# Last layer: one score and one peak side by side in TensorE's row halves, three PSUM banks for scores and four for peaks

## The reference, cut to what matters

```python
qkv = (x @ W_qkv + b_qkv).reshape(b, n, H, D, 3)          # b=64, n=1024, H=4, D=8
scores = jnp.einsum('bhnd,bhmd->bhnm', q, k) * scale
att = jax.nn.softmax(scores, axis=-1)
out = jnp.einsum('bhnm,bhmd->bhnd', att, v)
...                                                        # @ W_proj + b_proj, added to t
router_probs = jax.nn.softmax(x @ router_w + router_b, axis=-1)
top_p, top_i = jax.lax.top_k(router_probs, K)              # K=2 of 8 experts
```

## Time and profile before

| what | value |
|---|---|
| median of three runs | 6225.48 us (6224.43 to 6227.87) |
| the profiled execution, its own time | 6216.34 us |
| its span | 6214.5 us |
| mean granted TensorE clock | 0.956 |
| PE / DVE / ACT / POOL busy, whole span | 86% / 80% / 77% / 50% |

### The profile page before, as it was taken

The page is one execution under the profiler, slowest core; times in us unless marked ns, Lnnn a source line. Parts: engine busy times, 40 slices in busy tenths (PEclk is TensorE's granted clock), DMA queues, the critical chain, the costliest instruction groups (busy, mean ns, idle before and its releaser), DMA issues.

```text
span 6214.5 us, 145806 instructions
## 1 busy us (share of the span) xinstructions
PE 5346.4 (86%) x43064; PEld 2191.6 (35%) x43064; DVE 4957.7 (80%) x9330; ACT 4801.7 (77%) x8146; POOL 3128.8 (50%) x3692
## 2 busy tenths in 40 slices
PE   6649999999999998457999989998999899989997
PEld 5324444444444444442222222222222222222222
DVE  7837766767677675738999989999999899989995
ACT  1239989989899998215888888888888888888887
POOL 0037777777777776612444444444444344444443
PEclk9879999999999999677999999999999999999999
DMA  3010000000000000230000000000000000000000
GB/s 113 21 45 10 10 10 8 10 11 10 10 9 10 10 10 7 66 105 7 9 9 9 9 10 9 9 9 10 9 9 9 10 9 9 9 10 9 9 8 5
DMA packets 400111, 104.64 MB, mean 17 GB/s; under 512 B 348547, under 2 KB 398676, under 8 KB 398804
## 3 DMA queue, kind: packets, MB, share of 16 engines
q1 hardware_dynamic: 398163, 94.72, 7.1%
q10 hardware_dynamic: 1152, 0.05, 0.0%
HBM read 61.17 MB, written 33.56 MB: 15 GB/s over the span
## 4 chain that ended last, share of the span: by engine, by line
PE 24%; DVE 16%; issue 8%; ACT 3%; POOL 3%; DVEq 1%; DMA 0%; SPq 0%; ACTq 0%; POOLq 0%
DVE d_peaks L2296 12%; PE d_p_o L2124 7%; PE d_p_s L2111 5%; PE d_p_k L2140 5%; ACT d_wt L2007 2%; PE d_p_s L2213 2%; POOL d_rstd L1919 2%; PE d_p_s L2097 1%; PE d_p_s L2171 1%; PE d_p_s L2162 1%; DVE d_total L2306 1%; POOL d_xl L1923 1%; ACT d_answers L2003 1%; DVE d_rank L2388 1%; DVEq L2291 1%
## 5 line engine op out<-in xcount | busy, mean ns | idle before, releaser
L2296 DVE TENSOR_REDUCE d_peaks<-d_p_k 128x1 f32<-128x512 f32 x4096 | 2610.3, 683 | 242.8 <-PE d_p_k L2140 221.1
L2007 ACT ACTIVATE d_wt<-d_p_s 128x512 f32<-128x512 f32 x4096 | 2199.9, 616 | 416.0 <-PE d_p_s L2111 415.4
L771 ACT ACTIVATE b_wt<-b_sq 128x1024 f32<-128x1024 f32 (+3 forms) x1536 | 1240.0, 845 | 8.0 <-issue 8.0
L2124 PE MATMUL d_p_o<-d_wt,d_v_pad 128*32 128x512 f32 x8192 | 1095.5, 607 | 2.6 <-ACT d_o_sb L2012 1.9
L2140 PE MATMUL d_p_k<-d_kT,d_qT 64*128 64x512 bf16 x4096 | 800.8, 385 | 209.1 <-DVE d_peaks L2296 189.1
L680 POOL TENSOR_TENSOR b_sq<-b_sq 128x1024 f32<-128x1024 f32 (+1 forms) x512 | 849.6, 1680 | 234.4 <-DVE b_sq L995 234.4
L760 ACT ACTIVATE b_sq<-b_p_s 128x1024 f32<-128x1024 f32 (+2 forms) x1024 | 775.5, 757 | 180.2 <-PE b_p_s L831 173.3
L2111 PE MATMUL d_p_s<-d_qT,d_kT 64*128 64x512 bf16 x4096 | 801.4, 387 | 60.7 <-ACT d_wt L2007 40.4
L995 DVE TENSOR_TENSOR b_sq<-b_p_s,b_tri 128x1024 f32<-128x1024 f32 (+1 forms) x512 | 551.0, 1088 | 271.2 <-PE b_p_s L831 205.7
L1962 POOL TENSOR_TENSOR d_answers<-d_answers,d_mix 128x2048 f32<-128x2048 f32 x64 | 233.0, 3641 | 955.2 <-DVE d_mix L2397 955.2
L844 PE MATMUL b_p_o<-b_wt,b_v_pad 128*32 128x512 f32 (+2 forms) x6144 | 669.7, 508 | 1.9 <-ACT b_wt L771 1.0
(11 more groups left out here) (293 smaller groups left out, 7508.7 us busy)
## 6 DMA issues: line engine op xcount, KB each, us to landing
c_slots<-t SPq DMA_DIRECT2D x128, 128.0 KB, 2.5
a_xt<-in_x SPq DMA_DIRECT2D x4, 2048.0 KB, 14.7
a_w<-in_L_conv_W SPq DMA_DIRECT2D x64, 128.0 KB, 2.8
t<-a_rows SPq DMA_DIRECT2D x32, 256.0 KB, 2.4
b_x_in<-t SPq DMA_DIRECT2D x64, 128.0 KB, 2.7
t<-b_result SPq DMA_DIRECT2D x64, 128.0 KB, 2.2
t<-c_slots SPq DMA_DIRECT2D x64, 128.0 KB, 1.9
d_x_in<-t SPq DMA_DIRECT2D x64, 128.0 KB, 2.7
```

What stands on the lines that cost most here:

```text
L771: act.activation(wt[:, n % RING, :, 0:m], sq[:, n % SQ_RING, :, 0:m], ACT.Silu, scale=1.0 / D).then_inc(weighed, 1)
L2007: act.activation(wt[:, n % RING, :], tile(n)[:, :], ACT.Exp, scale=SCALE).then_inc(s_used, 1)
L2124: ins = pe.matmul(p_o[32 * h:32 * h + 32, :], v_pad[:, slot, kb, h, :], wt[:, (H * a + h) % RING, :], start=(kb == 0), stop=(kb == J - 1), ...
L2296: dve.tensor_reduce(peaks[:, m, r:r + 1], bank((m, r))[:, :], X, ALU.max).then_inc(k_used, 1)
```

## The change

Two constants change, and the order in which PE issues a half group. There are now three banks for scores and four for peaks. Instead of a pair of scores and then a pair of peaks, PE issues: a score in one row half, a peak in the other; a peak in the first row half, a score in the other. In each of the four, the wait is for that tile's own bank. The two peaks of one m swap their order (r = 1 first), on PE and on DVE. In the first half group of a window both scores stand ahead of the wait on `settled` and the peaks.

```diff
-S_BANKS, K_BANKS = 4, 3
+S_BANKS, K_BANKS = 3, 4
...
-        out += [(2 * a, 0), (2 * a, 1)] if "next" in on else []
+        out += [(2 * a, 1), (2 * a, 0)] if "next" in on else []
...
-                def scores(n):
+                def score(n):
                     qc, kb, h = UNITS[n]
-                    wait(pe, s_used, win.s_done(n + 1) - S_BANKS)
-                    for r in range(2):
-                        rows = slice(64 * r, 64 * r + 64)
-                        pe.matmul(seat(n + r)[:, :], kT[rows, win.slot("own"), h // 2, kb * P:(kb + 1) * P],
-                                  qT[rows, win.slot("own"), h // 2, qc * HALF:(qc + 1) * HALF],
-                                  start=True, stop=True).then_inc(s_made, 1)
+                    rows = slice(64 * (h % 2), 64 * (h % 2) + 64)
+                    pe.matmul(seat(n)[:, :], kT[rows, win.slot("own"), h // 2, kb * P:(kb + 1) * P],
+                              qT[rows, win.slot("own"), h // 2, qc * HALF:(qc + 1) * HALF],
+                              start=True, stop=True).then_inc(s_made, 1)
...
-                def peak(m):
+                def peak(m, r):
                     j, g, half = PEAKS[m]
+                    slot = win.slot("next")
+                    rows = slice(64 * r, 64 * r + 64)
+                    pe.matmul(free_bank((m, r))[:, :], qT[rows, slot, g, j * P:(j + 1) * P],
+                              kT[rows, slot, g, half * HALF:(half + 1) * HALF], start=True, stop=True).then_inc(k_made, 1)
+
+                def scores_and_peaks(n, m):
+
+                    if "own" in win.on:
+                        score(n)
                     if m == 0:
-                        arrived(s_used, win.settled)
-                    slot = win.slot("next")
-                    wait(pe, k_used, win.k_done((m, 1)) - K_BANKS)
-                    for r in range(2):
...
+                        if "own" in win.on:
+                            score(n + 1)
+                        if "next" in win.on:
+                            arrived(s_used, win.settled)
+                    if "next" in win.on:
+                        peak(m, 1)
+                        peak(m, 0)
+                    if "own" in win.on and m:
+                        score(n + 1)
...
                 for a in range(GROUPS):
-                    if "own" in win.on:
-                        scores(H * a)
-                    if "next" in win.on:
-                        peak(2 * a)
+                    scores_and_peaks(H * a, 2 * a)
                     for name in misc(K_MISC, a, win.on) + misc(S_MISC, a, win.on):
                         use_misc(name)
-                    if "own" in win.on:
-                        scores(H * a + 2)
-                    if "next" in win.on:
-                        peak(2 * a + 1)
+                    scores_and_peaks(H * a + 2, 2 * a + 1)
...
                 def peak(m):
-                    for r in range(2):
+                    for r in (1, 0):
                         dve.tensor_reduce(peaks[:, m, r:r + 1], bank((m, r))[:, :], X, ALU.max).then_inc(k_used, 1)
```

More of the change, by code:

```diff
@@ L1639, in k_order @@
     for a in range(GROUPS):
-        out += [(2 * a, 0), (2 * a, 1)] if "next" in on else []
+        out += [(2 * a, 1), (2 * a, 0)] if "next" in on else []
         out += misc(K_MISC, a, on)
-        out += [(2 * a + 1, 0), (2 * a + 1, 1)] if "next" in on else []
+        out += [(2 * a + 1, 1), (2 * a + 1, 0)] if "next" in on else []
     return out
@@ L2130, in free_bank @@
                     return p_k[win.k[name][1]]
-                def peak(m):
+                def peak(m, r):
                     j, g, half = PEAKS[m]
-                    if m == 0:
-                        arrived(s_used, win.settled)
-                    slot = win.slot("next")
-                    wait(pe, k_used, win.k_done((m, 1)) - K_BANKS)
-                    for r in range(2):
-                        rows = slice(64 * r, 64 * r + 64)
-                        pe.matmul(free_bank((m, r))[:, :], qT[rows, slot, g, j * P:(j + 1) * P],
-                                  kT[rows, slot, g, half * HALF:(half + 1) * HALF], start=True, stop=True).then_inc(k_made, 1)
+                    slot = win.slot("next")
[5 more added lines that the diff above has]
+                        score(n)
+                    if m == 0:
+                        if "own" in win.on:
[7 more added lines that the diff above has]
+                        score(n + 1)
                 def turn_o(i, half):
@@ L2444, in body @@
                     if "next" in win.on and m == PAIRS // 2:
-                        dve.wait_ge(k_used, win.k_done((PAIRS // 2 - 1, 1)))
+                        dve.wait_ge(k_used, win.k_done((PAIRS // 2 - 1, 0)))
                         shift_most(nx, 0)
```

## The result

The changed kernel takes 6241.4 us (median of 15 runs, 6233.7 to 6247.6) against 6224.5 us (15 runs): 1.0027 times the time before, 95% interval 1.0019 to 1.0035. I had forecast 6184 us. It is 17 us slower, and the sign was wrong.

What follows compares the result with a forecast made beforehand. Neither PE nor DVE was taken to bound everywhere. DVE's idle in three stretches was to fall from 3.46 to 2.8 us, gaining 0.66 a window, 41 us in all, giving 6184 us; 8-in-10 range 6055 to 6290.

Steps and rivals of the forecast that it cites:

- The bound: Last layer: neither PE nor DVE bounds everywhere; DVE idles 4.3 us a window, mostly waiting in three stretches of groups.
- the first stretch: Groups 3 to 5 (proj, qkv) of a window, where DVE was read as waiting 1.7 us in all.
- The peaks' cushion: Fourth peak bank and single waits let peaks come two reads earlier: 1.22 us gained at most per stretch where PE is slower.
- The experts: Groups 9 and 10: taking two of three score banks at once waits on the same half group; 2.5 us a window lost.
- One small tile to a group: Second half's second score waits 0.25 us more; counted only in groups 14 and 15, 0.5 us a window lost.
- Row halves: Score and peak matmuls paired across row halves: pairs falling apart cost 0, between -0.1 and +0.22 us for each wait.
- (c): Rival: gain and loss cancel, or the cushion is unused and earlier peaks offset the experts; 6225 us, chance 7%.
- (b): Rival: three score banks tie PE to ACT at each half group's second score; 73 us lost, 6298 us, chance 28%.
- the three stretches: Groups 3 to 5, 9 and 10, and 13 to 15, where DVE waited 1.7, 1.0 and 0.76 us a window.
- (a): Rival: the experts' loss and single waits stay hidden from DVE; 2.98 us a window gained, 6041 us, chance 17%.
- (d): Rival: the four matmuls, each with its wait, no longer start in pairs; over 6600 us, chance 2%.

Runs made afterwards that it cites:

- e1: The changed kernel with its new order but the banks of before, four for scores and three for peaks; 6149.7 us, 0.9882 times the kernel before.
- e9: The kernel before, pairs and banks as they were, but each of the four matmuls waits for its own bank only; 6178.8 us, ratio 0.9922.
- e10: As e1, four score and three peak banks, with the second score issued ahead of the second peak; 6142.5 us, 0.9865 times the kernel before.

## Why the prediction was wrong, step by step

**The bound.** Right. The gains and losses lie where the timelines had shown DVE waiting, and groups 11 and 12, where DVE is the slower one, kept their length to 0.01 us. One reading was wrong: of the first stretch's 1.7 us, the gap of 0.47 has DVE's own `d_total` as releaser, so PE's part was 1.24. The forecast gain of that stretch, 1.22, fits under either and does not change by it. And group 4 kept its length for another reason: its two gaps, 0.25 and 0.39, stand in the changed kernel as 0.28 and 0.39.

**The peaks' cushion.** "1.22 us of cushion, once for each stretch in which PE is the slower one": this step failed, and it alone turned the sign. The groups 0 to 3 gained 0.87 us (forecast 1.22 for the first stretch), the groups 13 to 15 gained 0.70 (forecast 0.72), and without the experts the whole change gained 6168.5 - 6044.0 = 124.5 us, 2.0 us a window, against 1.22 + 0.72 = 1.94 in the forecast. The third helping, at the experts, was not there. I reasoned that the lead "is built up while DVE is the slower one", and took the solid groups 5 to 8 for such. They are solid, but the ages of the tiles say that PE was hardly ahead in them. From a peak's matmul to its reduction, at the head of a group, the median is 0.6 to 0.7 us in groups 6 to 9, where 0.42 is the way there; at the head of group 9 it is 0.65, and was 0.56 before the change. In groups 1 and 2 it is 1.6 and 1.2 us, in groups 12 and 13 it is 1.7 and 2.1: there the lead exists, and pays for groups 2 and 3 and for groups 13 to 15. In the timeline of the changed kernel, group 13:

```profile
4432.31 0.60 PE L2134 MATMUL d_p_k<-d_kT,d_qT 64*128 64x512 bf16 x2
...
4432.87 1.29 DVE L2299 TENSOR_REDUCE d_peaks<-d_p_k 128x1 f32<-128x512 f32 x2
...
4433.62 0.39 PE L2134 MATMUL d_p_k<-d_kT,d_qT 64*128 64x512 bf16 x1
...
4434.21 0.39 PE L2134 MATMUL d_p_k<-d_kT,d_qT 64*128 64x512 bf16 x1 [0.21 <-DVE d_peaks L2299]
...
4434.30 0.38 PE L2109 MATMUL d_p_s<-d_qT,d_kT 64*128 64x512 bf16 x1
...
4434.44 1.88 DVE L2299 TENSOR_REDUCE d_peaks<-d_p_k 128x1 f32<-128x512 f32 x3
```

The two peaks of 4432.31 are the ones that DVE begins at 4434.44, 2.13 us later; the reductions at 4432.87 are of the pair before. Why groups 5 to 8 build no lead can be read from the starts of PE's scores, as medians over the full windows. From the first score of group 5 to that of group 9 PE takes 11.66 us, and DVE's reductions take 11.33 for the same four groups: DVE is solid there, but not the slower one. In groups 11 and 12 it is 6.03 for PE and 7.70 for DVE. With four score banks (e1) the four groups take PE 11.58, so three score banks in place of four explain 0.08 of it at most; how much of the 11.6 is PE's own work and how much its turns with ACT, no run separated. Put 0 for the cushion of that stretch, and the sum is +0.56 us a window instead of -0.66, against +0.41 in the table. In the whole launch that is +35 us where 17 were measured: the right sign, and twice the size.

**The experts.** The mechanism and the size held: +1.28 us a group and 2.5 a window forecast; by PE's starts 3.91 - 2.56 = 1.35 in group 9 and 3.90 - 2.98 = 0.92 in group 10, 2.27 together, and 2.14 for both by DVE's. The release of a bank for the bias took 0.24 us (the first read ends at 4417.49, the bias starts at 4417.73), not 0.1. In group 10 the loss was smaller, since the bias had waited there before as well: 0.97 us from first score to bias, where group 9 had 0.54.

**One small tile to a group.** The wait of +0.25 us is there: in groups 14 and 15 the second score of the second half starts 1.56 us after the group's first (forecast 1.61), and 1.32 with four score banks (e1; forecast 1.36 without the wait). DVE hardly sees it. By its reductions group 14 gained 0.39 us and group 15 lost 0.07, and the forecast for the stretch would have been 0.76 without this term and 0.72 with it, so the 0.70 measured does not test it. The bank swap without experts gains 0.7% with this wait in it.

**Row halves.** The price of 0 for pairs that fall apart holds in so far as no loss showed, but the gain beside it was missed. I had put the gain of not waiting for the later bank at up to 0.1 us for a wait; e9 and e1 show that the single waits give 49 us and the mixed order 25 more. Had the banks stayed, this would have been the change.

**Rivals.** (c), gain and loss cancel, is the nearest in number: 6225 against 6241, and gains of 1.7 us a window do stand against a loss of 2.14. It said no change, though, and the interval lies clear of 1. (b), slower since three score banks tie PE to ACT, has the sign right and its mechanism for one place, not for "the second score of each half group"; its price, 6298, was 57 us too high. That it decides from a cushion of 1.0 us fits: with 0 at the experts the average of the three stretches is at most (1.22 + 1.22 + 0) / 3 = 0.8. (a) was refuted by group 9's bias at 1.26 us, the sign that I had named; (d) by the pairs that start together.

## What to carry to other kernels

A bank moved from one pool to another has to be priced at the place that takes several at once: there the pool's size less the take is what counts, and three less two is one, a full round trip between the engines. A lead is worth something only if the stretch before lets it build up: ask how old the tiles are when the reader gets to them, before you spend it. And a wait for the later of two banks ahead of a pair is a cost to try to remove first; here that, with the order, gave 1.2% with no bank moved.

## What was not expected of the hardware

A score and a peak in different row halves start within 0.01 us of each other when both are free, also right after a switch from one `qT`/`kT` role to the other (4416.47 and 4416.48).

And a matmul that waits for its bank holds back one of the other row half that is written behind it. In the fence above, the peak in rows 0 to 63 waits for DVE until 4434.21, and the score in rows 64 to 127 behind it starts at 4434.30. Its row half was free from about 4433.84 (the peak of 4433.62, and 0.22 of occupancy), and the read that frees its bank had ended at 4433.82. One case could be chance, so I counted in the traces, half group by half group. In e1, windows 1 to 61, the second peak starts over 0.4 us behind the first in 369 half groups, and in all of them the second score starts at most 0.09 us behind that peak, never ahead. e10 writes this score ahead of this peak and changes nothing else: of its 548 half groups with such a late peak, the score starts ahead of it in every one, by 0.37 us in the median. So its bank and row half had been free, and the written order held it back. The Trainium skill, TensorE: Matmul & The Clock Gate, "Part 3: Packing small matmuls", has matmuls strictly first in, first out. By that rule the score waits as measured here; the trace agrees.
